# Four-stage transformer kernel: the second stage's weights and first batch are handled inside the first stage

## What is computed

```
x = x + ratio_attention(layernorm(x))    # 16 heads of 16; score = dot^2 / (|q|^2 + |k|^2 - 2 dot + eps), causal softmax
x = x + lowrank_ffn(layernorm(x))        # gelu(x U1 V1 + b1) U2 V2 + b2; U1 256x64, V1 64x1024, U2 1024x64, V2 64x256
x = x + zeroed_attention(layernorm(x))   # scores times a lower triangle mask, then softmax over all 512
x = x + ternary_ffn(layernorm(x))        # weights reduced to -1, 0, 1
```

## Time and profile before

| | |
|---|---|
| median of 3 runs | 2766.12 us (2760.79 to 2766.89) |
| profiled execution | 2765.75 us, of which the span of the trace is 2764.0 us |
| PE busy | 2609.7 us (94% of the span) |
| DVE, ACT, POOL busy | 2281.0, 2078.3, 1812.2 us |
| first stage | 0 to 1313.8 us |
| second stage | 1314.1 to 1589.0 us |
| third stage | from there to 2386.5 us |
| fourth stage | 2386.8 to 2764.0 us |

### The profile page before, as it was taken

The page is one execution under the profiler, slowest core; times in us unless marked ns, Lnnn a source line. Parts: engine busy times, 40 slices in busy tenths (PEclk is TensorE's granted clock), DMA queues, the critical chain, the costliest instruction groups (busy, mean ns, idle before and its releaser), DMA issues. The chain is left out here.

```text
span 2764.0 us, 75249 instructions
## 1 busy us (share of the span) xinstructions
PE 2609.7 (94%) x27002; PEld 1817.6 (66%) x27044; DVE 2281.0 (83%) x6936; ACT 2078.3 (75%) x3786; POOL 1812.2 (66%) x3152
## 2 busy tenths in 40 slices
PE   5999999999999999998789999999999999799999
PEld 3677777777777777777233367777777777566766
DVE  5999999999999999987555587888888887489998
ACT  4998899998989999987234366777676776578886
POOL 3766766776667667765332167776777777588885
PEclk8999999999999999999889999999999999899999
DMA  4334334443344344421200256565655553000001
GB/s 113 70 63 81 71 58 69 81 80 62 63 81 71 59 69 81 73 56 19 56 1 6 60 93 104 97 103 100 105 99 98 102 96 66 1 16 24 24 24 39
DMA packets 110387, 182.21 MB, mean 66 GB/s; under 512 B 27008, under 2 KB 96384, under 8 KB 97920
## 3 DMA queue, kind: packets, MB, share of 16 engines
q1 hardware_dynamic: 106560, 176.61, 34.8%
q10 hardware_dynamic: 3456, 0.79, 0.2%
HBM read 116.25 MB, written 60.29 MB: 64 GB/s over the span
## 5 line engine op out<-in xcount | busy, mean ns | idle before, releaser
L808 POOL TENSOR_TENSOR ratio_scores<-ratio_scores,ratio_max_cols 128x512 f32<-128x512 f32 (+3 forms) x1024 | 726.2, 726 | 319.4 <-DVE ratio_max_cols L718 317.3
L198 PE MATMUL bank<-ratio_k_stack,ratio_q_stack 102*128 102x512 bf16 (+7 forms) x2048 | 506.9, 303 | 33.0 <-DVE ratio_max_cols L718 17.3
L1379 DVE CUSTOM_DVE_ANT_0 zeroed_unused<-bank,zeroed_drop 128x512 bf16<-128x512 f32 (+3 forms) x1024 | 439.5, 484 | 104.5 <-PE bank L198 104.5
L718 DVE CUSTOM_DVE_ANT_0 ratio_scores<-bank,ratio_scores 128x512 f32<-128x512 f32 (+3 forms) x1024 | 472.5, 489 | 22.2
L1255 ACT ACTIVATE zeroed_prob<-bank 128x512 f32<-128x512 f32 x640 | 370.1, 593 | 151.6 <-PE bank L1148 150.4
L580 ACT ACTIVATE ratio_prob<-bank 128x512 f32<-128x512 f32 x640 | 378.4, 592 | 105.5 <-PE bank L494 102.9
L708 DVE TENSOR_TENSOR ratio_scores<-bank,ratio_inverse 128x512 f32<-128x512 f32 x640 | 435.9, 681 | 16.7 <-PE bank L198 9.6
L491 PE MATMUL bank<-const_f_sb,ratio_scores 128*128 128x128 f32 x2560 | 410.2, 274 | 0.9 <-ACT ratio_prob L580 0.9
L569 ACT ACTIVATE ratio_inverse<-bank 128x512 f32<-128x512 f32 x640 | 381.1, 596 | 12.7 <-PE bank L201 12.6
L573 ACT ACTIVATE ratio_inverse<-ratio_inverse 128x1024 f32<-128x1024 f32 x320 | 338.6, 1058 | 10.1
L1514 POOL TENSOR_SCALAR_AFFINE_SELECT zeroed_prob<-zeroed_prob 128x256 f32<-128x256 f32 (+1 forms) x640 | 227.5, 361 | 167.7 <-ACT zeroed_prob L1255 161.9
(11 more groups left out here) (218 smaller groups left out, 5443.5 us busy)
## 6 DMA issues: line engine op xcount, KB each, us to landing
ratio_q_stack<-ratio_parts_q SPq DMA_DIRECT2D x186, 128.0 KB
ratio_k_stack<-ratio_parts_k SPq DMA_DIRECT2D x186, 128.0 KB
zeroed_q_stack<-zeroed_parts_q SPq DMA_DIRECT2D x186, 128.0 KB, 4.7
zeroed_k_stack<-zeroed_parts_k SPq DMA_DIRECT2D x186, 128.0 KB, 7.5
ratio_parts_q<-ratio_parts SPq DMA_DIRECT2D x96, 128.0 KB
ratio_parts_k<-ratio_parts SPq DMA_DIRECT2D x96, 128.0 KB
zeroed_parts_q<-shared_parts SPq DMA_DIRECT2D x96, 128.0 KB
zeroed_parts_k<-shared_parts SPq DMA_DIRECT2D x96, 128.0 KB
```

The costliest lines, as they stand in the source:

```text
L198: i = e.matmul(bank[:, off:off + w], qs[0:rows, s, hh, ib * P:(ib + 1) * P], ks[0:rows, s, hh, 0:w], start=(k == 0), stop=mask is None, sk ...
L718: i = e.tensor_tensor_reduce(seg, dot_banks[n % 2][:, at], seg, 1.0, 0.0, ALU.mult, ALU.max, mx[:, pair % M_BUFS, c:c + 1])
L808: i = e.tensor_tensor(seg, seg, mx[:, pair % M_BUFS, c:c + 1].to_broadcast([P, w]), ALU.subtract)
L1379: i = e.tensor_tensor_reduce(unused[:, n % 2, at], bank[:, at], drop[:, L - (ib + 1) * P:L], 1.0, 0.0, ALU.add, ALU.max, mx[:, pair % FOLD ...
```

## The change

Three things change.

1. The second stage's start moves into the first stage. SP issues eight of the nine weight transfers (all but b2) at the end of its first-stage stream (`LowrankStart.load`). In the trailing slots, batch 0 is normalised (DVE, slots 640 and 641), turned (PE, 645 and 646), copied (DVE), multiplied by U1 (PE, 650) and copied (DVE). The scale of 15 batches comes from a logarithm and an exponential on ACT in slot 636, whose table is loaded already, in place of the square root and the reciprocal; the 16th batch's scale is made in the second stage at slot 56. The second stage's loop begins at once with `up(0)`.
2. A block of memory (`Arena`, 12 x 512 floats per partition) holds the first stage's parts, squares, transposed and normalised rows and outputs, then the second stage's weights and rows, then the third stage's `prob`. No tile changes size, apart from those that are no longer double.
3. The third stage's `FIRST_*` slots move: the first pair of row blocks is prepared from slot 630 on (turn at 637), where it was 638 (turn at 641); the second pair is normalised at slot 638, where it was 642, and turned at 645 as before.

The core of the diff:

```diff
+class Arena:
+    def __init__(self, net, ctx):
+        self.all = ctx.enter_context(net.nc.sbuf_tensor("arena", [P, 12 * L], F32))
+        at = lambda lo, n: self.all[:, lo * L:(lo + n) * L]
...
+        self.prob = self.all[:, :].rearrange("p (n t) -> p n t", t=L)
+    def load(self, e):          # LowrankStart: 2 x U1, 2 x V1, 2 x V2, U2, b1
...
+            def turn_early(pair):
+                q.wait_ge(ls["xn"], pair + 1)
+                q.wait_ge(s["maxima"], total)
+                turn_blocks(e, dot_banks[pair], lambda t: arena.rows[:, t, :], pair, net.ident).then_inc(ls["prep_filled"])
+            def rank_early():
+                q.wait_ge(ls["weights"], low.loaded)
+                q.wait_ge(ls["prep_read"], 2)
+                for c in range(2):
+                    i = e.matmul(dot_banks[0][:, :], arena.u1[:, c, :], arena.rows_T[:, c, :], start=(c == 0), stop=(c == 1))
+                i.then_inc(ls["prep_filled"])
...
+            def root_early():
+                cols = slice(0, EARLY_ROWS * T)
+                q.wait_ge(s["out_aggr"], 2 * EARLY_ROWS)
+                q.wait_ge(s["xn"], 2 * B)
+                e.activation(net.rstd[:, cols], net.mean_var[:, cols, 1], ACT.Ln, bias=net.eps_ln[:, :]).then_inc(s["log_var"])
+                q.wait_ge(s["log_var"], B + 1)
+                e.activation(net.rstd[:, cols], net.rstd[:, cols], ACT.Exp, scale=-0.5).then_inc(s["rstd"])
...
+            q.wait_ge(s["parts_q"], 48 * halves)
+            q.wait_ge(s["parts_k"], 48 * halves)
+            q.wait_ge(s["prep_filled"], ratio_prep(B - 1, "x1"))
+            low.load(e)
-FIRST_FLOOR, FIRST_ROOT, FIRST_SCALE = -6, -5, -4
-FIRST_XN, FIRST_TURN, FIRST_REST, FIRST_MID, FIRST_LO = (-2, 2), (1, 5), (2, 6), (3, 7), (4, 8)
+FIRST_FLOOR, FIRST_ROOT, FIRST_SCALE = -16, -14, -12
+FIRST_XN, FIRST_TURN, FIRST_REST, FIRST_MID, FIRST_LO = (-10, -2), (-3, 5), (-2, 6), (-1, 7), (0, 8)
-            turn_x(0, 0)
-            turn_x(0, 1)
-            rank(0)
-            e.activation(scale[:, :], net.mean_var[:, :, 1], ACT.Sqrt, bias=net.eps_ln[:, :]).then_inc(s["std"])
+            def last_root():
+                cols = slice(EARLY_ROWS * T, B * T)
+                e.activation(net.rstd[:, cols], net.mean_var[:, cols, 1], ACT.Ln, bias=net.eps_ln[:, :]).then_inc(s["std"])
+                q.wait_ge(s["std"], 1)
+                e.activation(net.rstd[:, cols], net.rstd[:, cols], ACT.Exp, scale=-0.5).then_inc(s["std"])
-            q.wait_ge(s["std"], 1)
-            e.reciprocal(scale[:, :], scale[:, :]).then_inc(s["scale"])
-            normal(0, 0)
-            normal(0, 1)
-            keep_x(0, 0)
-            keep_x(0, 1)
-            keep_rank(0)
```

More of the change, by code:

```diff
@@ L376, in ratio_attention @@
+def ratio_attention(net, w, x_dram, low):
     nc, B, L, D, T = net.nc, net.B, net.L, net.D, net.T
@@ L1051, in __init__ @@
         self.xnT = sb("xn_T", [P, 2, L])
-        self.xn, self.parts, self.rest = rows.xn, rows.parts, rows.rest
+        self.xn, self.parts, self.rest, self.prob = rows.xn, rows.parts, rows.rest, arena.prob
         self.values_ones = sb("v_ones", [P, STACKS, T, HALF, 32])
@@ L1070, in zeroed_attention @@
         values_ones, suffix, tails, drop, part_dram = start.values_ones, start.suffix, start.tails, start.drop, start.part_dram
-        prob = sb("prob", [P, FOLD_PROBS, L])
+        prob = start.prob
         o_group = sb("o_group", [P, L])
@@ L1630, in __init__, with lowrank_feed_forward @@
         self.down = sb("w_down_T", [P, FC, net.D])
-def lowrank_feed_forward(net, args, ternary, zeroed, start):
+def lowrank_feed_forward(net, low, ternary, zeroed, start):
     nc, B, L, D, T = net.nc, net.B, net.L, net.D, net.T
@@ L1664, in lowrank_feed_forward @@
             order.append(start_at[n])
-    prep = {use: i + 1 for i, use in enumerate(order)}
+    prep = {(0, "xa"): 1, (0, "xb"): 2, (0, "rank"): 3}
+    prep.update({use: i + 4 for i, use in enumerate(order)})
     post = lambda b, pair: 2 * b + pair + 1
@@ L2378, in two_layer_kernel @@
         net = Net(nc, ctx, B, L, D)
+        arena = Arena(net, ctx)
+        low = LowrankStart(net, ctx, arena, {k: a[f"L0_ffn_{k}"] for k in ("U1", "V1", "b1", "U2", "V2", "b2")})
         with ExitStack() as first:
@@ L2383, in two_layer_kernel @@
             load_start(net, first, a["L0_attn_x"], a["const_f"], a["const_b"], ratio)
-            ratio_attention(net, ratio, a["L0_attn_x"])
+            ratio_attention(net, ratio, a["L0_attn_x"], low)
         ternary = TernaryWeights(net, ctx, {k: a[f"L1_ffn_{k}"] for k in ("w_up", "w_down")})
@@ L2391, in two_layer_kernel @@
         with ExitStack() as second:
-            start = ZeroedStart(net, second, rows)
-            lowrank_feed_forward(net, {k: a[f"L0_ffn_{k}"] for k in ("U1", "V1", "b1", "U2", "V2", "b2")}, ternary, zeroed, start)
+            start = ZeroedStart(net, second, rows, arena)
+            lowrank_feed_forward(net, low, ternary, zeroed, start)
             zeroed_attention(net, zeroed, start, rows)
```

123 lines of the change are left out of this document (81 added, 42 removed).

## The result

The changed kernel takes 2746.82 us in the median of four runs (2740.75 to 2749.42), the kernel before 2765.01 beside it. The ratio is 0.9933, with a 95% interval of 0.9913 to 0.9953. The profiled execution is the shortest of the four: 2740.75 us, a span of 2739.0 against 2764.0. That difference of 25 us is not what the change is worth, and much of what follows is about telling the two apart.

A forecast was written before the change was run, and what follows sets the result against it. PE's own work was taken as the bound (busy 94%), with gains only where PE idles. -11.6 + 0.4 + 0.5 - 3.0 = -13.7 us off 2765.75 gave 2752.05, 2752.4 for a median; range 2747 to 2758.

The forecast's parts named there:

- Part 1: Second stage's start: 14.4 us of waiting removed, 2.8 us added to the first stage's tail, loop 11.6 us earlier.
- early turns and U1, up to the last group's turn: First stage's tail: two early turns add 1.1 us, U1's matmuls in slot 650 add 1.4 us.
- ACT's root in slot 636: First stage's tail: two ACT instructions over 60 columns add 0.3 us, bounds 0 and 0.6.
- clock at the opening, V1 to the second U1: Second stage's opening: PE still idles 2.5 us, so the clock falls again and costs 0.4 us.
- the clock stays up: Rival, second stage's opening: the clock doesn't fall there, 1.4 us less, 2751 us; chance 0.12.
- Part 3: Third stage's last slots: POOL waits and low clock go, 5.9 us; costs come back; net gain 3.0 us.
- Part 3 gives nothing: Rival, third stage's end: PE's waits only move, term 0 to +1.5 us, time 2755.4 to 2756.9; chance 0.20.
- Part 2: Second stage, slot 56: ACT makes the 16th batch's scale while PE waits for it, +0.5 us, bounds 0 and 0.8.
- Part 4: Shared memory block: only addresses change, 0 us, with 1 us on both sides.
- gather held up: Rival, end of SP's first-stage stream: new weight transfers delay the last gather, 4.5 us more, 2756.9; chance 0.02.
- doesn't do what it says: Rival, second stage's opening: the loop's first product has another late input, time 2760 or above; chance 0.04.
- slower: Rival, shared block: third stage's `prob` lies elsewhere and costs time per unit, slower than before; chance 0.04.

The follow-up runs named there:

- square of filled kernels: Kernel before, third-stage slots only, opening only and changed kernel, each with unread filler matmuls in the first and third stages' tails: 2758.2, 2755.2, 2745.3, 2741.6 us.
- the two corners that ran side by side: With fillers in both tails: kernel before with only the FIRST_* slots moved, 2755.2 us, and the changed kernel, 2741.6 us.
- e1: Kernel before with only the third stage's FIRST_* slots moved: 2759.1 +- 0.8 us.
- e8: A kernel with the new opening; the text doesn't tie this label to an edit or a time.
- e10: Changed kernel with the first pair of the fourth stage's rows normalised in slot 631 instead of 630: 2748.2 +- 0.9 us.
- e2: Changed kernel with the old third-stage FIRST_* slots: 2749.4 +- 1.6 us.

## Why the prediction was right in kind and too small in size

The forecast lay 5.8 us above the changed kernel's mean (2752.4 against 2746.6). Two errors of the same sign make it up, and each is a step of the prediction that failed.

**The base, 3.1 us.** The step is "2765.75 - 13.7 = 2752.05 for it, and 2752.4 us for a median": I took the sum off one profiled execution and set it 0.37 below the median of three runs, 2766.12. The mean of 91 runs is 2763.1 +- 0.3. Three runs 6 us apart tell their centre to 2 us at best, and the profile was one of the slower ones: in its second profile the same kernel was 5.9 us shorter. With the right base the same terms give 2749.4 and a range of 2744 to 2755, and the measured 2746.8 lies in it. This is the larger error, and the one that is fully shown. It says nothing against the chains and waits that I had named.

**The size, 2.8 +- 1.1 us, in Part 1.** The step is the sum -11.6 + 0.4 + 0.5 = -10.7 us. The square of filled kernels has 13.2 +- 0.7 in its place (13.6 +- 0.9 by the two corners that ran side by side). Term by term, forecast, the first pair of profiles, and what the other profiles say:

| term | forecast | first pair | other profiles |
|---|---|---|---|
| time from DVE's last instruction to V1 | -14.4 | -14.8 (15.11 to 0.33) | old 14.33 to 15.11 in five profiles, mean 14.70; new 0.33: -14.4 |
| early turns and U1, up to the last group's turn | +2.5 | +2.2 (3.25 to 5.46) | the same |
| ACT's root in slot 636 | +0.3 | 0.0 (12.46 and 12.48 between two landmarks of the last slots, from 1286.27 and 1285.09) | read in this pair only |
| from the group's turn to the stage's end | 0 | +0.1 (10.73 to 10.83) | 12.3 to 14.2 where the clock falls in a projection: old `e1`; new `e8`, `e10`, `e2` |
| clock at the opening, V1 to the second U1 | +0.4 | -0.5 (9.51 to 9.02) | old 9.51 or 8.55; new 9.02 to 10.18 in five without fillers, 8.55 with |
| slot 56 | +0.5 | +0.4 | read in this pair only |
| sum | -10.7 | -12.6 | |

- Two terms were too large by 0.3 us each, the early turns with U1 and ACT's root. That much is clear, and it is the smaller part.
- The term of the clock is where the rest lies if PE is kept busy: with fillers V1 to the second U1 takes 8.55 us against 9.51, so the term is -1.0 for a forecast of +0.4. The rival "the clock stays up" describes that pair.
- In the kernels as they stand the rows don't show the term wrong. The first pair has -0.5, but the very same opening took 9.10 us in the changed kernel's second profile and 10.18 in `e2`, and the old one 8.55 in its second profile:

```profile
1317.50 3.79 PE L1840 MATMUL bank<-arena 64*128 64x512 f32 x8 [2.13 <-PEq L1003]
```

- Over the whole stretch from the last score turn to the second U1 the three profiles with the old opening and no fillers have 38.2 us in the mean (37.3 to 38.8), the five with the new one 27.7 (25.6 to 30.2). That is 10.1 us less, slot 56 taken in, about the forecast. The times of the same kernels say 13.7 (`e2`). Eight single executions that scatter by 2 us can't settle this, and why the times give 2 to 3 us more than the forecast stays open.
- I also read PE's idle time at the old opening too high: 10.9 us from 1311.99 to V1, not 12. The fourth stage's 0.70 us as a model for the opening was too long by 0.4: the distance depends on the block (0.33 here). The old opening's 15.11 us was the longest of five, which makes up for it.

**Part 3** came out at 3.4 +- 0.7 us for a forecast of 3.0, but the inside of the sum was different. Gone were both waits, as said. The new wait in slot 634 was 1.81 us, not 1.1 (I had not thought of DVE's late scale), the low part in slot 640 cost nothing (no wait in slot 644, 0.8 forecast), ACT cost 0.70 us in slot 641 (0.5 forecast), the turn in slot 637 0.43 from its start to the next (0.5). By rows the stretch is 3.7 us shorter where the clock stays up (31.52 to 27.82) and 2.1 us where the new wait makes it fall (29.41). "The clock stays 1.00 in slots 641 and 645" was right for those slots and missed that my own new wait would do in slot 634 what the old one did in 645.

**Part 2** cost 0.4 us for 0.5. **Part 4** cost nothing that a row shows: attending matmuls 1.08 us and triangles 0.29 us from the shared block, as from the old buffers. **The gather** was not held up: its transfers are ahead of the weights on SP, the weights landed at about 1260, 42 us ahead of U1's matmuls at 1302.30, and slot 617's first product waited for nothing.

**The rivals**: "Part 3 gives nothing", "gather held up", "doesn't do what it says" and "slower" are out. "The clock stays up at the opening" came true in some executions and not in others, as the sentence on the freely running window had it. The signs I had named came in: V1 0.3 us behind DVE (0.7 said), DVE's end at 1314.95 (1316.6 said, of which about 1.2 us is the start of the run, see below), no table load before the gelu's, slots 641 and 645 without a wait for POOL.

## What to carry to other kernels

Take the base from as many runs as there are, and price a term by the stretch between two landmarks that the edit doesn't touch, at the same clock on both sides: such stretches agreed to 0.1 us between executions, where no transfer was waited for, while whole times scattered by 3.3. One pair of profiles doesn't price a term that hangs on the clock: the same opening took 9.02 and 10.18 us. Where a profile shows the clock low beside short waits of PE, cover those waits with matmuls that nobody reads before you compare two kernels: here it took the scatter from 3.3 to about 2 us, helped to separate the parts of the change, and was itself worth 4 to 5 us. A wait that is removed by moving work ahead of another user of the same engine comes back there; ask whether the new wait is long enough to cost what the old one did.

## What I had not expected of the hardware

- The clock at the start of a run is drawn too. Three of the profiles had the second group of the first stage's four first projections at 1.98 or 1.99 us and the first score matmul at 38.8 to 39.2 us, the others at 2.7 to 3.8 us and 40.2 to 41.9. One of the three is the first profile of the changed kernel: 1.9 us of its lead over the kernel before was there at that point. Twelve other profiles with the same code up to there don't have it, so it isn't the change's.
- The granted clock's column can't be trusted up to the first change that it records. In one profile it reads 1.00 over the first 50 us, while four matmuls that take 1.99 us at the full clock took 3.78:

```profile
21.36 3.78 PE L491 MATMUL bank<-arena,ratio_w_in 128*128 128x512 f32 x4 [2.21 <-DVE arena L757]
```

```profile
20.00:30.00 10.00, 5.71 (x8) 1.39 (x8) 2.40 (x5) 2.38 (x4) 2.30 (x2) 1.00 0.13 39
```

So the sums of low clock in my expectations hold only from about 60 us on (about 80 us and 40 us in the first profiles of the two kernels); the duration of a known matmul is the better witness.
